# A two-layer attention kernel on one core: a new order of steps, set by new places in its calendar

## What is computed

```python
def reference(x, ctx_1024, _lenS2, ...):
    x = x + _L0_xattn_ref(_layernorm(x, axis=-1), ctx_1024, ctx_1024, _lenS2, Wq, Wk, Wv, Wo)
    x = x + _L0_ffn_ref(_layernorm(x, axis=-1), gw1, ..., ob)
    return x
```

## Time and profile before

| | |
|---|---|
| median of three runs | 1425.97 us |
| lowest and highest | 1421.93 and 1426.45 us |
| profiled execution, first to last instruction | 1426.7 us |
| TensorE busy | 1391.0 us |
| VectorE, ScalarE, GpSimd busy | 951.9, 861.3, 679.8 us |
| mean granted TensorE clock | 0.980 of 2.4 GHz |

### The profile page before, as it was taken

How to read it: one execution, slowest core, us unless ns; L and a number is a source line. 1 busy time by engine, 2 the same in 40 slices (tenths; PEclk the granted TensorE clock), 3 DMA queues, 4 the chain that set the end, 5 groups by cost and what they waited for, 6 DMA issues and landing times.

```text
span 1426.7 us, 17122 instructions
## 1 busy us (share of the span) xinstructions
PE 1391.0 (97%) x5704; PEld 702.4 (49%) x5704; DVE 951.9 (67%) x1687; ACT 861.3 (60%) x1499; POOL 679.8 (48%) x411
## 2 busy tenths in 40 slices
PE   8998999999999999999999999999999999999987
PEld 5545444545455444555555445455545454444432
DVE  4454577766767677767777677767777677666572
ACT  2425474866577663975658664876648665565652
POOL 2011143545555362556445463555625455465675
PEclk9889999999999999999999999999999999999999
DMA  7514233522434224522234224332235323233210
GB/s 252 143 53 133 46 68 96 153 76 46 98 110 108 75 54 125 137 61 76 68 111 123 75 59 135 110 85 67 58 104 152 76 46 97 64 101 79 81 39 30
DMA packets 78767, 130.81 MB, mean 92 GB/s; under 512 B 26374, under 2 KB 32134, under 8 KB 75607
## 3 DMA queue, kind: packets, MB, share of 16 engines
q1 hardware_dynamic: 74007, 128.55, 33.4%
q10 hardware_dynamic: 4672, 1.17, 0.4%
HBM read 66.08 MB, written 12.21 MB: 55 GB/s over the span
## 4 chain that ended last, share of the span: by engine, by line
PE 85%; ACT 7%; issue 2%; DMA 2%; POOL 2%; DVE 1%; ACTq 0%; SPq 0%; POOLq 0%
PE pj L1217 43%; PE scT L1302 9%; PE sc L1274 8%; PE acc L1331 7%; PE sc L1263 4%; PE pj L1247 2%; PE pj L1311 2%; PE scT L1295 2%; PE pj L1319 2%; PE pj L1340 2%; DMA qs<-shift 2%; PE pj L1190 1%; ACT xhat L810 1%; PE pj L1202 1%; PE pj L1211 1%
## 5 line engine op out<-in xcount | busy, mean ns | idle before, releaser
L925 ACT ACTIVATE probs<-scT 128x512 f32<-128x512 f32 x512 | 288.9, 594 | 303.9 <-PE scT L1302 300.8
L1048 DVE TENSOR_REDUCE negmax<-sc 128x1 f32<-128x512 f32 x512 | 338.0, 684 | 140.7 <-PE sc L1274 139.7
L784 POOL TENSOR_TENSOR probs_sum<-probs_sum,probs 128x1024 f32<-128x1024 f32 x128 | 300.2, 2365 | 57.4 <-ACT probs L925 57.3
L1075 DVE RECIPROCAL inv_sum<-pj 128x128 f32<-128x128 f32 x256 | 225.0, 921 | 59.9 <-PE pj L1340 39.2
L1274 PE MATMUL sc<-ks,qs 96*128 96x512 f32 x512 | 260.1, 541 | 2.4 <-DVE negmax L1048 1.6
L1217 PE MATMUL pj<-XT,Wqk 128*128 128x512 f32 x512 | 257.3, 598 | 0.6 <-DVE Wqk L1140 0.6
L1302 PE MATMUL scT<-qs,ks 99*128 99x512 f32 x512 | 250.9, 517 | 6.2 <-DMA qs<-shift 3.2
L780 POOL TENSOR_TENSOR probs_sum<-probs 128x1024 f32<-128x1024 f32 x64 | 151.4, 2372 | 173.8 <-ACT probs L925 173.8
L790 POOL TENSOR_TENSOR uv_stack<-UVS_sb,uv_stack 96x1024 fp32r<-96x1024 f32 x32 | 75.7, 2367 | 178.1 <-ACT UVS_sb L832 178.1
L1302 PEld LDWEIGHTS scT<-qs,ks 99*128 99x128 f32 x512 | 94.7, 191 | 124.5 <-ACT probs L925 60.4
L754 POOL TENSOR_TENSOR xhat<-xhat,inv_sum 128x128 f32<-128x128 f32 (+1 forms) x56 | 45.1, 806 | 207.7 <-DVE inv_sum L1075 207.7
(11 more groups left out here) (103 smaller groups left out, 1716.6 us busy)
## 6 DMA issues: line engine op xcount, KB each, us to landing
Wqk<-in_WmT SPq DMA_DIRECT2D x16, 1024.0 KB, 6.1
Wvo<-in_WmT SPq DMA_DIRECT2D x16, 1024.0 KB, 6.5
UVS_sb<-in_UVS SPq DMA_DIRECT2D x64, 192.8 KB, 3.4
qs<-stage_lo SPq DMA_DIRECT2D x136, 64.0 KB, 2.2
qs<-qs SPq DMA_DIRECT2D x34, 256.0 KB, 3.0
X<-in_x SPq DMA_DIRECT2D x8, 1024.0 KB, 6.0
ks<-stage_lo SPq DMA_DIRECT2D x128, 64.0 KB, 2.0
ks<-ks SPq DMA_DIRECT2D x32, 256.0 KB, 3.0
```

The costliest lines, as they stand in the source:

```text
L784: nc.gpsimd.tensor_tensor(probs_sum[:, pair], probs_sum[:, pair], probs[:, kt % 2, pair], ALU.add)\
L925: nc.scalar.activation(probs[:, kt % 2, jj, :], scT[:, ST[step], :], ACT.Exp, scale=SCALE)\
L1048: nc.vector.tensor_reduce(negmax[:, 0, n:n + 1], sc[:, SC[step], :], AX.X, ALU.max, negate=True)\
L1075: nc.vector.reciprocal(inv_sum[:, INV[use], at], pj[:, PJ[left_in(full)], at])\
```

## The change

All numbers of `PERIOD`, `CALENDAR` and `OWN` are replaced. The set of steps is the same, and no function changes. The new numbers are about fifty times larger, which alone does nothing, since they only sort. A cut of the diff:

```diff
-PERIOD = 2034
+PERIOD = 101700
 CALENDAR = {
-    "deviation": (-1817, 90),
-    "normalize": (-1775, 138),
-    "xpose": (-1734, -1732, -1712, -1710, 141, 141, 163, 163),
+    "deviation": (-94823, 3442),
+    "normalize": (-89000, 4557),
+    "xpose": (-86872, -86470, -85785, -85617, 5627, 6269, 8161, 9438),
...
-    "pick": (326,),
+    "pick": (13782,),
...
-    "residual_bias": (1404,),
+    "residual_bias": (153263,),
...
-    "pv": (1586, 1615, 1860, 2110, 2174, 2226, 2359, 2380, 2589, 2596, 2735, 2911, 3110, 3268, 3376, 3426),
+    "pv": (79278, 80952, 93776, 105024, 106614, 112817, 118095, 120724, 129751, 129975, 137637, 137730, 156825,
+        157625, 170361, 171137),
...
-    "den": (1871, 2376, 2959, 3434),
+    "den": (93678, 120397, 146187, 172250),
...
 OWN = {
-    "context_keys": {(0, 0): -11084, (1, 0): -10576, (2, 0): -9150, (3, 0): -8881, (0, 1): -8717, (1, 1): -8570,
-        (2, 1): -1258, (3, 1): -1209},
+    "context_keys": {(0, 0): -493264, (1, 0): -488361, (2, 0): -467354, (3, 0): -442885, (0, 1): -265916,
+        (1, 1): -254524, (2, 1): -194707, (3, 1): -128204},
...
-    "xpose": {(0, 0, 0): -8403, (0, 0, 1): -8371, (0, 0, 2): -8329, (0, 0, 3): -8320, (0, 1, 0): 148, (0, 1, 1): 149,
+    "xpose": {(0, 0, 0): -617117, (0, 0, 1): -563632, (0, 0, 2): -509792, (0, 0, 3): -496115, (0, 1, 0): 7263,
...
-    "den": {(7, 0): 18507, (7, 1): 19738, (7, 2): 20740, (7, 3): 21892},
+    "den": {(7, 0): 902335, (7, 1): 1017624, (7, 2): 1227375, (7, 3): 1482034},
```

More of the change, by code:

```diff
@@ new lines @@
+    "context": (-97613,),
+    "context_v": (-81730,),
+    "load": (-99291,),
+    "stats": (-97647, -96492, -96130, -95962),
+    "deviation": (-94823, 3442),
+    "normalize": (-89000, 4557),
+    "xpose": (-86872, -86470, -85785, -85617, 5627, 6269, 8161, 9438),
+    "q1": (-84498, -83804, -83614, -82231, -82200, -81018, -80078, -79435, -44638, -44337, -43479, -42501, -37323,
+        -37099, -35638, -33505),
+    "q1_split": (-81366, -74908, -41498, -31104),
+    "q1_rows": (-80365, -58593, -39649, -21412),
@@ new lines @@
+    "residual1": (-2301, -1173, 1516, 3111),
+    "residual_bias": (153263,),
+    "token_sums": (7059, 7908, 8523, 9496),
+    "gate_hidden": (11318,),
+    "gate_top": (12774,),
+    "gate_scale": (14376,),
+    "uv_hi": (19985, 24673, 32055, 148114),
+    "uv_lo": (21783, 28547, 33735, 152657),
+    "weff": (22045, 22262, 22366, 23519, 29340, 30053, 30307, 30516, 36153, 36760, 37281, 41683, 164962, 166232,
+        168046, 170341),
+    "qk": (24289, 24785, 26148, 26803, 32252, 32327, 33400, 34197, 58749, 60144, 60637, 61438, 62030, 63088, 63240,
+        63934, 72404, 72886, 73803, 75035, 84298, 85050, 85511, 87236, 105715, 106658, 108940, 111740, 113996,
+        114599, 115141, 115535),
@@ new lines @@
+    "qk_split": (27556, 35465, 63741, 64620, 79506, 88470, 112691, 117045),
+    "qk_rows": (37602, 36640, 65263, 69029, 98795, 89411, 118481, 119180),
+    "qk_stack": (43831, 37311, 71065, 71270, 98952, 98661, 122510, 122595),
+    "v": (39115, 39228, 42662, 43393, 39212, 41278, 43567, 44442, 48092, 48591, 50945, 52382, 49844, 51527, 53101,
+        53197),
+    "v_bias": (44002, 45928, 52497, 54244),
[5 rows of a table added]
+    "shift": (65364, 95688, 119861, 145872),
+    "shift_move": (67209, 101826, 120043, 146893),
[7 rows of a table added]
@@ new lines @@
+    "weff": {(7, 3, 0): 1129666, (7, 3, 1): 1152643, (7, 3, 2): 1350211, (7, 3, 3): 1385160, (0, 0, 0): 21649,
[14 rows of a table added]
+    "load": {(0,): -1060048},
+    "stats": {(0, 0): -939019, (0, 1): -892853, (0, 2): -837512, (0, 3): -756961},
+    "deviation": {(0, 0): -702219, (0, 1): 4015, (7, 1): 715397},
+    "normalize": {(0, 0): -628852, (0, 1): 5970, (7, 1): 716381},
+    "xpose": {(0, 0, 0): -617117, (0, 0, 1): -563632, (0, 0, 2): -509792, (0, 0, 3): -496115, (0, 1, 0): 7263,
[12 rows of a table added]
+    "csc": {(0, 0, 0): -259232, (0, 0, 1): -256579, (0, 0, 2): -245137, (0, 0, 3): -237843, (0, 1, 0): -202832,
[5 rows of a table added]
@@ L255 @@
+    "mask": {(): -556137},
+    "key_rows": {(0,): -684430, (1,): -405988},
 }
```

172 lines of the change are left out of this document (75 added, 97 removed), and 207 rows, old and new, of tables (CALENDAR, OWN).

## The result

The new places make the kernel **slower: 1478.16 us** (1473.66 to 1482.36, four runs) against 1425.08 us (1421.93 to 1426.45), a ratio of 1.0376 with a 95% interval of 1.0350 to 1.0402. The prediction, 1408.2 us with a range up to 1421, is wrong by 70 us, and the sign is wrong too.

What follows compares the result with a forecast made beforehand. TensorE, busy 1391.0 of 1426.7 us, was taken as the bound. Savings of 1.0 us (start), 6.6 (five periods) and 10.2 (end) gave 1408.9 us profiled, 1408.2 us as median, range 1396 to 1421.

Steps and rivals of the forecast that it cites:

- the bound above: Inside each period, the allowance for waits left uncounted: 1.2 us less to 1.6 us more a period.
- the end: Behind the last period: fewer narrow runs and less GpSimd idle time before its last sums, 10.2 us less.
- the waits inside a period: Around each period's transposes: about 1.4 us of new wait for the low-rank factor replaces some 1.7 us; counted as nothing.
- the third transpose's wait: In each period, TensorE's 0.66 us idle while ScalarE's copy is late; should go as the deviation steps move ahead.
- the start: Before the first period: element 0's transposes go ahead of key projections; 1 us less, ends 8 more and 7 less.
- the five periods: Five equal TensorE stretches of about 164 us; four fewer narrow runs in each save 1.32 us, 6.6 us in all.
- Rival 1: Behind each period's transposes, ScalarE's queue becomes the bound: TensorE waits 4 us more a period, 1432 us; chance 0.07.
- Rival 2: In the periods, the 1.3 us saved in each comes back as waits: 1415 us; chance 0.13.
- Rival 5: On TensorE, width changes are cheap and the 0.33 us an artefact of modelled ends: 1415 us; chance 0.05.
- narrow run: Consecutive TensorE steps of 32 weight columns; entering costs 0.14 us, leaving 0.19; the change has 31 fewer, 10.2 us.
- rival 4: At the start, dense work leaves no half-clock stretch: 6 us less than counted, 1402 us; chance 0.14.

Runs made afterwards that it cites:

- run 4: The kernel before the change with only the 1 MB query and key loads (last element: value too) moved late, just ahead of the stack transfers: 1476.65 us, ratio 1.0381.
- run 1: The changed kernel with only SyncE's 1 MB query and key loads (last element: value too) put back in their old order: 1441.34 us, ratio 1.0119.
- 12: The changed kernel, no place moved, with ScalarE making the gate's broadcast and mean and variance corrected one column at a time: 1466.61 us, ratio 1.0300.
- 14: The changed kernel with loads back, gate later, end's transfers and two period places moved, and mean and variance corrected in single columns: 1414.02 us, ratio 0.9923.
- runs 6 to 11: The changed kernel with loads back and gate 0.7 us later, then variants moving end transfers, splitting narrow runs or moving other places: 1422.53 to 1441.70 us.
- run 8: The changed kernel with loads back, gate 0.7 us later and end's transfers moved, plus nine narrow steps of each period set apart: 1441.70 us, ratio 1.0122.
- 13: The changed kernel with loads, gate, end and two period places repaired, plus ScalarE's broadcast and single-column corrections of mean and variance: 1414.71 us, ratio 0.9928.
- run 7: The changed kernel with loads back, gate 0.7 us later and the last element's transfers and second gate step moved: 1425.15 us, ratio 0.9991.

## Why the prediction was wrong

**The step that failed** is "SyncE's choice of experts now stands ahead of the first two 1 MB weight loads ... two of them fit. I cost both at nothing". It saw the move, and asked only who waits for the loads: VectorE, 14 us later. That was right, since no wait for `Wqk` appeared. It did not ask who is behind them: the stack transfers in SyncE's own queue and the shift's 16 KB from ScalarE's, which TensorE needs at once. The earlier trace rows gave the load's 6.1 us; two of them in front of a transfer that took 2 to 4 us was the sum to make (in run 4 the DMA engines are 0.93 busy for 16 us). The fallback, "the price is part of the bound above" of 1.6 us a period, was too small by a factor of three (run 1 takes 5.5 us off each period) and left out the end, where the value load joins them. Undoing it gave 37 us of the 53, doing it alone, closer to the shift, cost 53.

**The second step** is the waits inside a period. That the deviation moved ahead was counted as pure gain: the third transpose's wait did go, as forecast. But the new place lies over GpSimd's sums, and the earlier trace rows showed neither GpSimd beside VectorE at that point nor the operation in company. Together with the broadcast it cost 11.5 us in the changed kernel (12); alone it cost some 8 us in the repaired one (14, less what the form itself may give). With both repaired the medians lie 10 us apart, of the 18 forecast. In the profiled executions, which lie further apart (1426.7 and 1409.1 us), the start is 3.2 us shorter, the five periods 8.2 and the end 6.2, where 1.0, 6.6 and 10.2 were forecast: only the end falls short.

**The rivals.** Rival 1 (slower, 0.07) named the place, the shift behind the transposes, but put it to ScalarE's queue; ScalarE issued 0.7 us behind the transpose. It also priced it at 4 us a period where 7.6 came. Rival 2 (the saving comes back as waits) described runs 6 to 11 well, and 14 showed that one of these waits, for the maxima, had its cause in the held correction. Rival 5 (cheap width changes) is out by run 8.

**What held.** 0.33 us a narrow run (its rows give 0.13 and 0.19): measured 0.34 over all, 0.36 in the periods. Periods of 162.5 us: 162.2 in 13 and 14, once the two collisions are gone; TensorE is busy for 806.6 us in 14's five periods, 8.2 less than before, where 6.6 were forecast. The start: TensorE's first rows,

```profile
18.12 3.60 PE L1241 MATMUL pj<-ident_sb,xhat 128*128 128x128 f32 x16 [11.65 <-ACT xhat L840]
21.55 8.46 PE L1220 MATMUL pj<-probs,Wqk 128*128 128x308 f32 x32
...
30.29 1.88 PE L1247 MATMUL pj<-XT,Wq_sb 128*128 128x512 f32 x4
```

stand where they were put (18.1, four projections, 30); the clock from 58 to 82 us was 1.00, which is rival 4's mark, though the start gave 3.6 us less and not 7. A half-clock stretch from 11.3 to 21.5 us now reaches over the transposes, where the kernel before had a shorter one; the clock from 18 to 30 us is 0.85 in place of 1.00, some 2 us.

**The end** was off as well. From the transpose of element 7's third head group to the last product the forecast was 50.3 us; it took 64.8 (1408.88 to 1473.7), and 60.9 in run 7. The transpose and GpSimd's first sums of the last two head groups, in the changed kernel:

```profile
1408.88 0.30 PE L1310 MATMUL pj<-ident_sb,negmax 128*128 128x128 f32 x1
```

```profile
1422.90 4.72 POOL L810 TENSOR_TENSOR probs_sum<-probs 128x1024 f32<-128x1024 f32 x2 [6.42 <-ACT probs L955]
...
1441.71 4.67 POOL L810 TENSOR_TENSOR probs_sum<-probs 128x1024 f32<-128x1024 f32 x2 [2.94 <-PE pj L1370]
```

From transpose to first sum it took 14.0 us, not 9.4, and 13.8 in run 7 with the transfers mended. The forecast took it from the old order (9.7). Between the two stand a `den` and `pv` steps, as before, but now one `pv` more, and behind the late shift transfer a stretch at half clock falls on them: that `den` alone took 1.93 us. GpSimd's idle time before the last sums stayed at 2.9 us (forecast: under 1), now because it waited for `den`, which stood behind the very score steps that were to feed it. How the rest of the end divides was not tried.

## What to carry to other kernels

When a large transfer moves, look behind it and not only ahead: list every transfer that is issued, from any engine, while its bytes are in flight, and who waits for each. When a step moves, lay its time over the other engines' rows too; an operation that was 0.2 us alone can last as long as a neighbour's, and the profile then calls it busy. If a repaired order refuses its saving, and each wait that is removed comes back elsewhere, compare the mean time of every group of operations before and after, before moving more steps.

## What the runs showed of the hardware

- A 16 KB transfer lands after 2.0 to 3.6 us with no large load in the 10 us ahead of it, 2.9 to 5.5 with 1 MB and 5.3 to 8.3 with 2 MB from another queue.
- VectorE's small scalar operations last up to 2.45 us when they start inside a sum of GpSimd of 2.35 us, and 0.17 to 0.29 otherwise; on single columns 0.15 us, inside the sums or not. The mean's correction, right behind the held one, kept its 0.16 us.
- A wait of 4.94 us before TensorE was followed by 4 us at clock 0.50; waits of 0.2 to 1.2 us at the gate's small matmuls were followed by a fall too, while the old order's wait of 0.66 us before the third transpose was not. What tells them apart was not tried.
- Entering and leaving a narrow run costs about 0.35 us: 0.34 over 49 more of them, 0.36 of TensorE's busy time over the 40 in the periods.
